# Sliding-window attention: the second query tile's two masked triangles in one block of probabilities

## The chip, the cores and the metric

The kernel runs on one core of a Trainium2 chip. The metric is the device time of one execution in microseconds. Before the change it is 873.5 us, the median of 3 runs (873.45 to 874.37).

## The reference

Layer norm, then grouped-query attention times the silu of a feed-forward block, added to the input. The attention is what the change touches (4 batches of 256 tokens, 32 query heads, 8 KV heads, width 128, window 128):

```python
q = _rope((x @ wq).reshape(B, S, 32, 128), pos)
k = _rope((x @ wk).reshape(B, S, 8, 128), pos)
v = (x @ wv).reshape(B, S, 8, 128)
scores = jnp.einsum('bqhgd,bshd->bhgqs', qg, k) * sm_scale
allowed = (j <= i) & (j > i - 128)
attn = jax.nn.softmax(jnp.where(allowed, scores, neg), axis=-1)
out = jnp.einsum('bhgqs,bshd->bqhgd', attn, v).reshape(B, S, 32 * 128)
return out @ wo
```

A batch is two query tiles of 128. For the first only its own keys count, on and below the diagonal. For the second the keys of the first tile count above the diagonal (the far triangle) and its own on and below it. The two triangles are complementary: together they fill one 128x128 block.

## The kernel before, in words

Five engines run programs of their own, joined by semaphores; the order in each is written out by hand. The feed-forward block takes the first 225 us. Then 8 KV groups follow; a group is two **steps**, one for each pair of batches: `step(g, 0)`, called even below, and `step(g, 1)`, called odd. Groups 1 to 6 are a hardware loop; groups 0 and 7 have small differences, and the last step (`not more`) an order of its own.

Matrix products are exact to nearly 32 bits: an operand is split in a high part (ScalarE, fp32r) and the low rest (VectorE or GpSimd, a subtraction), and `three` (L975) makes three matmuls of each pair.

A step does, for its pair (`b` is the batch in it):
- **the projections of the step to come** (`project`, L1074): 0 is k, 1 is v, 2 to 5 are the four query heads, 12 matmuls each. Rotary embedding of part c: ScalarE swaps halves (`halves`, L482), VectorE multiplies by the cosine (`cos_part`, L788), GpSimd multiplies by the sine and adds (`sin_part`, L316), ScalarE and VectorE split (`kq_hi`, L491; `kq_lo`, L799). On ScalarE and VectorE these stand between the parts of the attention.
- **scores** (L1095): for each head 128x128 for the first tile, 128x256 for the second, in one bank, [own | far, near]. `masking` (L808) takes one bank at a time, adds masks, scales and finds the extreme in two fused operations; `exps` (L512) is on ScalarE; `normalise` (L826) multiplies by the reciprocal sums on VectorE. `scores` of head s waits until head s-2 is masked.
- **turns** (`p_turn`, L1108): the probabilities of four heads are transposed, block by block (r = 0, 1, 2) into a bank; ScalarE copies the high part to `ph[r]` (`p_hi`, L528) and VectorE subtracts the low part `pl[r]` (`p_lo`, L835). The first turn of a batch waits for `probs_done` of all four heads.
- **attend** (L1126): output tile 0 is V0 x block 0, output tile 1 is V0 x block 1 + V1 x block 2. Then `o_hi`, `o_lo` (L534, L846) split the output.
- **out_project** (L1142): 12 matmuls for each of 4 token tiles, into the two banks that `attend` used too. The first waits until `o_lo` of output tile 2 has read its bank. `accumulate` (L852) adds to the running sum.

Queue order decides. Around the change it is: TensorE: turns (0,0) (0,1), projection 0, turn (0,2), projection 1, attend 0, scores, projection 2, scores, turn of V, projections 3 and 4 with turn (1,0) ahead of 4's last part, turn (1,1), projection 5 with turn (1,2) inside, attend 1, scores of the next step, output projections. ScalarE, late in the step: `halves(3)`, `p_hi(1,1)`, `kq_hi(1)`, `p_hi(1,2)`, `kq_hi(2)`, `halves(4)`, `kq_hi(3)`, `o_hi(2)`, `o_hi(3)`, `kq_hi(4)`, exponentials. GpSimd: `sin_part(0)`, in an even step four splits of `wo`, `sin_part(1..4)`, in an even step six splits of the next group's input weights (`lo_in`). Loads go through a ring of 5 slots that these splits set free.

## Time and profile before

| what | value |
|---|---|
| median of 3 runs | 873.5 us |
| the profiled execution | 874.13 us |
| its span, first to last instruction | 872.3 us |
| TensorE busy | 840.8 us (96%) |
| VectorE / ScalarE / GpSimd busy | 597.1 / 472.3 / 390.2 us |
| transposes of `probs` (L1122) | 384 |

Busy time is a sum over instructions. Matmuls overlap: one of 512 columns is shown with 0.39 us, but the next begins 0.23 us after it, so pitches are read from start to start. In the loop all steps of a kind last the same to 0.02 us, so one of each is enough. An idle time stands in brackets behind a row, with the engine that ended it. A row of a stretch reads: from:to, length, then busy us and number of instructions for PE (TensorE), PEld (its weight loads), DVE (VectorE), ACT (ScalarE) and POOL (GpSimd), then the granted clock as a share of 2.4 GHz, the share of the DMA engines and GB/s.

### The profile page before, as it was taken

Reading aid. Unit: us, or ns where it says so; the run is one execution under the profiler, and the core shown is the slowest. Engines: PE = TensorE matmul, PEld = TensorE weight load, DVE = VectorE, ACT = ScalarE, POOL = GpSimd, SP = SyncE. Lnnn points to the kernel's source line nnn. Section 1 sums busy time; section 2 is a strip of 40 time slices with the busy share of each in tenths; the row PEclk is TensorE's granted clock in tenths of the full one; section 3 lists DMA queues with packets and bytes.
Section 4 is the critical chain, followed back from the end, with each engine's and each line's share of the span. In section 5 each row is a group of like instructions: output and inputs, shape, how many; then the busy total and the mean of one; then the engine's idle time right before and its main releaser. Section 6 shows DMA issues by size and latency. Waiting matters only on the chain.

```text
span 872.3 us, 13995 instructions
## 1 busy us (share of the span) xinstructions
PE 840.8 (96%) x4252; PEld 702.3 (81%) x4252; DVE 597.1 (68%) x1615; ACT 472.3 (54%) x1139; POOL 390.2 (45%) x303
## 2 busy tenths in 40 slices
PE   3999999999989999999999999999999999999987
PEld 3777888888767888888888888888888888888876
DVE  7953554433569676876868596777759686866794
ACT  2474121132667557574757575475747566664742
POOL 0144121124545536551744454275525545641893
PEclk9999999999999999999999999999999999999989
DMA  6200001002010201200120102012001201100121
GB/s 195 57 15 10 12 25 46 24 1 72 1 31 19 74 0 49 65 10 1 48 72 0 48 19 54 0 48 72 0 4 44 72 0 48 49 23 0 49 62 72
DMA packets 40224, 32.55 MB, mean 37 GB/s; under 512 B 5056, under 2 KB 32384, under 8 KB 40192
## 3 DMA queue, kind: packets, MB, share of 16 engines
q1 hardware_dynamic: 40192, 32.16, 13.0%
q8 instruction: 16, 0.26, 0.1%
q14 instruction: 16, 0.13, 0.0%
HBM read 30.05 MB, written 2.10 MB: 37 GB/s over the span
## 4 chain that ended last, share of the span: by engine, by line
PE 86%; DVE 6%; ACT 3%; issue 2%; POOL 2%; DMA 0%; SPq 0%; ACTq 0%; DVEq 0%; POOLq 0%
PE bank L982 26%; PE bank L984 25%; PE bank L983 25%; PE bank L1122 5%; PE bank L1102 3%; DVE probs L831 1%; ACT W2raw L434 1%; POOL acc L338 1%; PE bank L1092 1%; PE bank L1002 1%; DVE xl L667 1%; POOL swap L321 1%; DMA xn<-in_L_attn_x 0%; POOL q L325 0%; ACT W2h L435 0%
## 5 line engine op out<-in xcount | busy, mean ns | idle before, releaser
L321 POOL TENSOR_TENSOR swap<-swap,cst 128x512 f32<-128x512 f32 x80 | 103.7, 1296 | 251.1 <-ACT swap L489 249.8
L982 PE MATMUL bank<-xh,wih 128*128 128x512 f32 x384 | 158.0, 411 | 0.2 <-DVE q L795 0.2
L984 PE MATMUL bank<-xh,wil 128*128 128x512 f32 x384 | 150.7, 393 | 0.0
L983 PE MATMUL bank<-xl,wih 128*128 128x512 f32 x384 | 150.0, 391 | 0.0
L516 ACT ACTIVATE probs<-probs,nmx 128x128 f32<-128x128 f32 (+1 forms) x256 | 113.5, 444 | 36.5 <-DVE nmx L816 36.1
L831 DVE TENSOR_SCALAR probs<-probs,rinv 128x128 f32<-128x128 f32 x250 | 125.4, 544 | 4.4
L532 ACT ACTIVATE ph<-bank 128x512 fp32r<-128x512 f32 x96 | 55.7, 598 | 109.5 <-PE bank L1122 108.1
L982 PE MATMUL bank<-woh,oh 128*128 128x512 f32 x256 | 101.1, 395 | 0.0
L983 PE MATMUL bank<-wol,oh 128*128 128x512 f32 x256 | 100.5, 393 | 0.0
L984 PE MATMUL bank<-woh,ol 128*128 128x512 f32 x256 | 100.5, 393 | 0.0
L287 POOL TENSOR_TENSOR hl<-act_h,hh 128x512 fp32r<-128x512 f32 x22 | 29.9, 1363 | 148.1 <-ACT hh L417 148.1
L325 POOL TENSOR_TENSOR q<-q,swap 128x512 f32<-128x512 f32 x64 | 89.3, 1396 | 8.1 <-DVE q L795 3.8
L837 DVE TENSOR_TENSOR pl<-bank,ph 128x512 fp32r<-128x512 f32 x96 | 64.6, 687 | 40.4 <-ACT ph L532 40.2
L984 PEld LDWEIGHTS bank<-xh,wil 128*128 128x128 f32 x384 | 72.1, 188 | 16.0
L305 POOL TENSOR_TENSOR wil<-raw,wih 128x512 fp32r<-128x512 f32 x48 | 61.1, 1305 | 51.1 <-ACT wih L471 51.1
L983 PEld LDWEIGHTS bank<-xl,wih 128*128 128x128 f32 x384 | 72.5, 189 | 11.8
L982 PEld LDWEIGHTS bank<-xh,wih 128*128 128x128 f32 x384 | 72.3, 188 | 12.0 <-DVE q L795 0.6
L816 DVE CUSTOM_DVE_ANT_0 probs<-bank,cst 128x128 f32<-128x128 f32 (+1 forms) x256 | 76.3, 349 | 5.1 <-issue 5.1
L982 PE MATMUL bank<-xh,W13h 128*128 128x512 f32 x176 | 70.5, 401 | 3.4 <-DVE W13l L692 2.4
L848 DVE TENSOR_TENSOR ol<-bank,oh 128x512 fp32r<-128x512 f32 x64 | 43.3, 687 | 40.4 <-ACT oh L537 40.4
L984 PE MATMUL bank<-xh,W13l 128*128 128x512 f32 x176 | 69.2, 393 | 0.0
L983 PE MATMUL bank<-xl,W13h 128*128 128x512 f32 x176 | 68.7, 391 | 0.0
(103 smaller groups left out, 1832.3 us busy)
## 6 DMA issues: line engine op xcount, KB each, us to landing
raw<-in_L_attn_wq SPq DMA_DIRECT2D x32, 256.0 KB, 2.9
raw<-in_L_attn_wo SPq DMA_DIRECT2D x32, 256.0 KB, 2.9
packed<-in_L_ffn_w SPq DMA_DIRECT2D x20, 128.0 KB, 2.1
xn<-in_L_attn_x SPq DMA_DIRECT2D x8, 256.0 KB, 3.4
raw<-in_L_attn_wk SPq DMA_DIRECT2D x8, 256.0 KB, 3.0
raw<-in_L_attn_wv SPq DMA_DIRECT2D x8, 256.0 KB, 2.6
raw<-in_L_attn_x SPq DMA_DIRECT2D x8, 256.0 KB, 2.8
out<-gate SPq DMA_DIRECT2D x8, 256.0 KB, 2.0
```

The source lines that it names most:

```text
L305: nc.gpsimd.tensor_tensor(lo, raw[:, slot, :], hi.bitcast(f32), ALU.subtract).then_inc(wl_done, 1)
L321: nc.gpsimd.tensor_tensor(v, v, spread(sin.unsqueeze(1), P, 2, SEQ), ALU.mult).then_inc(sin_done, 1)
L325: nc.gpsimd.tensor_tensor(dst, dst, swap[:, s, :], ALU.add).then_inc(rope_done, 1)
L516: e = nc.scalar.activation(probs[:, s, c0:c1], probs[:, s, c0:c1], ACT.Exp, bias=nmx[:, s, i:i + 1], scale=-1.0, accum_out=rsum[:, s, i:i ...
L532: nc.scalar.activation(ph[:, r, :], T_B[(7 * bp + j) % 2][:, :], ACT.Copy).then_inc(ph_done, 1)
L816: m = nc.vector.tensor_tensor_reduce(out=probs[:, s, c0:c1], in0=S_B[s % 2][:, c0:c1], in1=mask[:, c0:c1], scale=-SM, scalar=TOP, op0=ALU. ...
L831: m = nc.vector.tensor_scalar(probs[:, s, c0:c1], probs[:, s, c0:c1], rinv[:, s, i:i + 1], None, ALU.mult)
L837: nc.vector.tensor_tensor(pl[:, r, :], T_B[(7 * bp + 4 * b + r) % 2][:, :], ph[:, r, :].bitcast(f32), ALU.subtract).then_inc(pl_done, 1)
L982: nc.tensor.matmul(out_, sh, mh, start=(i == 0), stop=False)
L983: nc.tensor.matmul(out_, sh, ml, start=False, stop=False)
L984: m = nc.tensor.matmul(out_, sl, mh, start=False, stop=(i == n - 1))
L1122: i = nc.tensor.transpose(T_B[(7 * bp + j) % 2][:, h * P:(h + 1) * P], probs[:, 4 * b + h, r * P:(r + 1) * P], ident)
```

## The change

The scores of the second tile are merged before masking: with a predicated copy the far block's scores are written over the near block's wherever the key's index in its tile is above the query's, in PSUM. Softmax, normalise and turn then deal with one block of 128 columns instead of 256. A step has four turns instead of six. Since the one block P holds far and near, the output is taken as V0 x P + (V1 - V0) x (P kept where near): V's second tiles are stored as the difference `vd`, and GpSimd multiplies `ph[1]` and `pl[1]` with a 0/1 mask (`near`) to give block 2. `attend` still has nine matmuls for a batch; before the last three it waits for `kept`.

The order changes too: turn (1,0) goes ahead of part 1 of projection 4 (it was ahead of part 3) and turn (1,1) ahead of its part 3; on ScalarE `p_hi(1,1)` goes ahead of `halves(3)`; GpSimd gets `near(0)` at the start of the step and `near(1)` between `sin_part(2)` and `sin_part(3)`; the first two of the six input splits go ahead of `halves(4)` and `sin_part(4)`. In the last step GpSimd has `near(0)`, `rest(3)`, `rest(4)`, `near(1)` and then the old order. The diff, cut to its core:

```diff
+        causal, plain, far, keep = [cst[:, C_MASK + n * P:C_MASK + (n + 1) * P] for n in range(4)]
+        ident = cst[:, C_ID:C_ID + P]
...
-        probs = sb("probs", [P, 2 * GH, 3 * P], f32, main)
+        probs = sb("probs", [P, 2 * GH, 2 * P], f32, main)
+        vd = sb("vd", [P, 2, HD], f32, main)
...
+            def near(g, bp, b):
+                m = spread(keep.unsqueeze(1), P, GH, P)
+                for p_, s_, out_ in ((ph, ph_done, ph), (pl, pl_done, pl)):
+                    pool.wait_ge(s_, cnt(4, g, bp, 2 * b + 2))
+                    wait(pool, o_ps, cnt(4, g, bp, 2 * b))
+                    nc.gpsimd.tensor_tensor(out_[:, 2, :].rearrange("p (h n) -> p h n", h=GH),
+                                            p_[:, 1, :].bitcast(f32).rearrange("p (h n) -> p h n", h=GH), m,
+                                            ALU.mult).then_inc(kept, 1)
...
+                near(g, bp, 0)
...
-                for c in range(1, 5):
-                    sin_part(ng, nbp, c)
+                sin_part(ng, nbp, 1)
+                sin_part(ng, nbp, 2)
+                near(g, bp, 1)
+                sin_part(ng, nbp, 3)
+                if nxt:
+                    lo_in(g + 1, 0)
+                    lo_in(g + 1, 1)
+                sin_part(ng, nbp, 4)
                 if w and last:
-                    for t in range(4):
+                    for t in range(3):
                         rest(t)
                 if nxt:
-                    for c in range(6):
+                    for c in range(2, 6):
...
+                wait(act, vdl_done, cnt(1, g, bp, 0))
+                tiles = t_bank[:, :].rearrange("p (t n) -> p t n", n=HD)
+                nc.scalar.activation(vd[:, :, :], tiles[:, 1::2, :], ACT.Copy)
+                nc.scalar.activation(vh[:, bp, 0::2, :], tiles[:, 0::2, :], ACT.Copy).then_inc(vh_done, 1)
+            def vd_hi(g, bp):
+                act.wait_ge(vd_done, cnt(1, g, bp, 1))
+                nc.scalar.activation(vh[:, bp, 1::2, :], vd[:, :, :], ACT.Copy).then_inc(vdh_done, 1)
...
-                for r in range(3):
+                for r in range(2):
...
+                v_hi(ng, nbp, T_B[(5 * bp + 2) % 2])
                 halves(ng, nbp, 2)
                 kq_hi(ng, nbp, 0)
+                vd_hi(ng, nbp)
                 p_hi(g, bp, 1, 0)
+                p_hi(g, bp, 1, 1)
                 halves(ng, nbp, 3)
-                p_hi(g, bp, 1, 1)
                 kq_hi(ng, nbp, 1)
-                p_hi(g, bp, 1, 2)
                 kq_hi(ng, nbp, 2)
+                if nxt:
+                    hi_in(g + 1, 0)
+                    hi_in(g + 1, 1)
...
             def masking(g, bp, b, h0):
-                wait(dve, pT_ps, cnt(6, g, bp, 3 * b - 3))
+                wait(dve, pT_ps, cnt(4, g, bp, 2 * b - 2))
                 for h in (h0, h0 + 1):
                     s = 4 * b + h
+                    own, both = S_B[s % 2][:, 0:P], S_B[s % 2][:, 2 * P:3 * P]
                     dve.wait_ge(scores_ps, cnt(8, g, bp, s + 1))
-                    nc.vector.memset(pace[:, s:s + 1], 0.0)
-                    for i, (c0, c1) in enumerate(((0, P), (P, 3 * P))):
+                    nc.vector.memset(pace[:, 2 * s:2 * s + 1], 0.0)
+                    nc.vector.copy_predicated(both, far.bitcast(i32), S_B[s % 2][:, P:2 * P]).then_inc(merged, 1)
+                    dve.wait_ge(merged, cnt(8, g, bp, s + 1))
+                    nc.vector.memset(pace[:, 2 * s + 1:2 * s + 2], 0.0)
+                    for i, (src, add) in enumerate(((own, causal), (both, plain))):
                         m = nc.vector.tensor_tensor_reduce(
-                            out=probs[:, s, c0:c1], in0=S_B[s % 2][:, c0:c1], in1=mask[:, c0:c1], scale=-SM,
-                            scalar=TOP, op0=ALU.add, op1=ALU.min, accum_out=nmx[:, s, i:i + 1])
+                            out=probs[:, s, i * P:(i + 1) * P], in0=src, in1=add, scale=-SM, scalar=TOP,
+                            op0=ALU.add, op1=ALU.min, accum_out=nmx[:, s, i:i + 1])
                     m.then_inc(masked, 1)
...
             def v_lo(g, bp, t_bank):
+                tiles = t_bank[:, :].rearrange("p (t n) -> p t n", n=HD)
                 dve.wait_ge(vh_done, cnt(1, g, bp, 1))
-                nc.vector.tensor_tensor(vl[:, bp].rearrange("p t n -> p (t n)"), t_bank[:, :],
-                                        vh[:, bp].rearrange("p t n -> p (t n)").bitcast(f32),
+                nc.vector.tensor_tensor(vd[:, :, :], vd[:, :, :], tiles[:, 0::2, :], ALU.subtract).then_inc(vd_done, 1)
+                nc.vector.tensor_tensor(vl[:, bp, 0::2, :], tiles[:, 0::2, :], vh[:, bp, 0::2, :].bitcast(f32),
                                         ALU.subtract).then_inc(vl_done, 1)
+            def vd_lo(g, bp):
+                dve.wait_ge(vdh_done, cnt(1, g, bp, 1))
+                nc.vector.tensor_tensor(vl[:, bp, 1::2, :], vd[:, :, :], vh[:, bp, 1::2, :].bitcast(f32),
+                                        ALU.subtract).then_inc(vdl_done, 1)
...
+                    v_lo(ng, nbp, T_B[(5 * bp + 2) % 2])
                     cos_part(ng, nbp, 2)
                     kq_lo(ng, nbp, 0)
                     p_lo(g, bp, 1, 0)
+                    p_lo(g, bp, 1, 1)
+                    vd_lo(ng, nbp)
                 cos_part(ng, nbp, 3)
-                p_lo(g, bp, 1, 1)
                 kq_lo(ng, nbp, 1)
-                p_lo(g, bp, 1, 2)
                 kq_lo(ng, nbp, 2)
...
             def p_turn(g, bp, b, r, last):
-                j = 4 * b + r
+                j = 3 * b + r
                 if r == 0:
                     pe.wait_ge(probs_done, cnt(8, g, bp, 4 * b + 4))
-                if j == 5:
+                if j == 4:
                     if last:
-                        pe.wait_ge(pl_done, cnt(6, g, bp, 2))
+                        pe.wait_ge(pl_done, cnt(4, g, bp, 1))
                     else:
                         pe.wait_ge(vl_done, cnt(1, g, bp, 2))
                 else:
-                    wait(pe, pl_done, cnt(6, g, bp, {0: -1, 1: 0, 2: 1, 4: 3, 6: 4}[j]))
+                    wait(pe, pl_done, cnt(4, g, bp, {0: -1, 1: 0, 3: 2}[j]))
                     if j == 1:
                         pe.wait_ge(vl_done, cnt(1, g, bp, 1))
                 for h in range(GH):
-                    i = nc.tensor.transpose(T_B[(7 * bp + j) % 2][:, h * P:(h + 1) * P],
+                    i = nc.tensor.transpose(T_B[(5 * bp + j) % 2][:, h * P:(h + 1) * P],
                                             probs[:, 4 * b + h, r * P:(r + 1) * P], ident)
                 i.then_inc(pT_ps, 1)
...
+                pe.wait_ge(vdl_done, cnt(1, g, bp, 1))
...
-                    pe.wait_ge(pl_done, cnt(6, g, bp, 3 * b + (1 if t == 0 else 3)))
+                    pe.wait_ge(pl_done, cnt(4, g, bp, 2 * b + t + 1))
                     three(O_B[j % 2][:, :], [(vh[:, bp, 2 * b + kt, :], vl[:, bp, 2 * b + kt, :],
-                                              ph[:, r, :], pl[:, r, :]) for r, kt in blocks]).then_inc(o_ps, 1)
+                                              ph[:, r, :], pl[:, r, :]) for r, kt in blocks],
+                          {1: lambda: pe.wait_ge(kept, cnt(4, g, bp, 2 * b + 2))}).then_inc(o_ps, 1)
...
-                p_turn(g, bp, 0, 2, not more)
-                if not begun:
                     project(ng, nbp, 1)
                 attend(g, bp, 0)
...
-                    pe.wait_ge(pl_done, cnt(6, g, bp, 2))
-                    v_turn(ng, nbp, T_B[(7 * bp + 3) % 2])
+                    pe.wait_ge(pl_done, cnt(4, g, bp, 1))
+                    v_turn(ng, nbp, T_B[(5 * bp + 2) % 2])
                     project(ng, nbp, 3)
-                    project(ng, nbp, 4, {3: lambda: p_turn(g, bp, 1, 0, False)})
-                p_turn(g, bp, 1, 1, False)
-                project(ng, nbp, 5, {2: lambda: p_turn(g, bp, 1, 2, False)})
+                    project(ng, nbp, 4, {1: lambda: p_turn(g, bp, 1, 0, False),
+                                         3: lambda: p_turn(g, bp, 1, 1, False)})
+                project(ng, nbp, 5)
                 attend(g, bp, 1)
...
-    for n, ok in enumerate((j <= i, j > i, j <= i)):
-        c[:, C_MASK + n * P:C_MASK + (n + 1) * P] = np.where(ok, 0.0, NEG)
+    for n, block in enumerate((np.where(j <= i, 0.0, NEG), np.zeros((P, P)), j > i, i <= j)):
+        c[:, C_MASK + n * P:C_MASK + (n + 1) * P] = block
```

## Rows read from the trace of the kernel before

**Rows 1.** The page's first part: busy us, share of the span, instructions.

```profile
PE 840.8 (96%) x4252; PEld 702.3 (81%) x4252; DVE 597.1 (68%) x1615; ACT 472.3 (54%) x1139; POOL 390.2 (45%) x303
```

**Rows 2.** An odd and an even step: span, busy by engine (count), clock.

```profile
524.28:563.83 39.55, 39.55 (x208) 33.60 (x209) 27.98 (x90) 22.29 (x59) 15.62 (x12) 1.00 0.09 25
563.83:603.22 39.39, 39.39 (x208) 33.12 (x205) 30.86 (x89) 27.48 (x69) 23.73 (x19) 1.00 0.15 41
```

**Rows 3.** Timeline of TensorE around a turn: start us, us, engine, line.

```profile
546.28 0.39 PE L984 MATMUL bank<-xh,wil 128*128 128x512 f32 x1
546.51 0.60 PE L1122 MATMUL bank<-cst,probs 128*128 128x128 f32 x4
...
547.18 0.40 PE L983 MATMUL bank<-xl,wih 128*128 128x512 f32 x1
```

**Rows 4.** Timeline of TensorE, the same odd step: five places.

```profile
537.16 0.38 PE L1102 MATMUL bank<-k,q 128*128 128x128 f32 x2
...
542.18 0.39 PE L982 MATMUL bank<-xh,wih 128*128 128x512 f32 x1
...
543.55 0.60 PE L1122 MATMUL bank<-cst,probs 128*128 128x128 f32 x4
...
551.59 0.39 PE L982 MATMUL bank<-woh,oh 128*128 128x512 f32 x1
...
555.05 0.36 PE L982 MATMUL bank<-kh,qh 128*128 128x256 f32 x1
```

**Rows 5.** Timeline of VectorE, the same odd step.

```profile
537.94 0.29 DVE L816 CUSTOM_DVE_ANT_0 probs<-bank,cst 128x128 f32<-128x128 f32 x1 [0.78 <-issue]
...
538.52 0.29 DVE L816 CUSTOM_DVE_ANT_0 probs<-bank,cst 128x128 f32<-128x128 f32 x1
...
539.07 0.69 DVE L795 TENSOR_TENSOR q<-bank,cst 128x512 f32<-128x512 f32 x1
...
539.87 1.58 DVE L831 TENSOR_SCALAR probs<-probs,rinv 128x128 f32<-128x128 f32 x2
...
542.22 0.55 DVE L831 TENSOR_SCALAR probs<-probs,rinv 128x128 f32<-128x128 f32 x2
...
550.70 0.69 DVE L848 TENSOR_TENSOR ol<-bank,oh 128x512 fp32r<-128x512 f32 x1 [0.24 <-ACT oh L537]
```

**Rows 6.** One line's instructions: count, then duration ns min/median/max.

```profile
L816 DVE CUSTOM_DVE_ANT_0 probs<-bank,cst x256: 278/352/422, 243.2 to 844.8; 128x128 f32<-128x128 f32 x128
```

**Rows 7.** Timeline of GpSimd, the odd step and the start of the even one.

```profile
540.00 1.29 POOL L325 TENSOR_TENSOR q<-q,swap 128x512 f32<-128x512 f32 x1
543.11 1.30 POOL L321 TENSOR_TENSOR swap<-swap,cst 128x512 f32<-128x512 f32 x1 [1.81 <-ACT swap L489]
544.49 1.62 POOL L325 TENSOR_TENSOR q<-q,swap 128x512 f32<-128x512 f32 x1
546.24 1.30 POOL L321 TENSOR_TENSOR swap<-swap,cst 128x512 f32<-128x512 f32 x1
547.62 1.38 POOL L325 TENSOR_TENSOR q<-q,swap 128x512 f32<-128x512 f32 x1
...
572.47 5.05 POOL L305 TENSOR_TENSOR wol<-raw,woh 128x512 fp32r<-128x512 f32 x4
```

**Rows 8.** Timeline of ScalarE, the odd step.

```profile
542.44 0.60 ACT L489 ACTIVATE swap<-bank 64x512 f32<-64x512 f32 x1
...
544.18 0.60 ACT L532 ACTIVATE ph<-bank 128x512 fp32r<-128x512 f32 x1 [0.49 <-PE bank L1122]
...
549.76 0.42 ACT L496 ACTIVATE qh<-q 128x256 fp32r<-128x256 f32 x1
```

**Rows 9.** Two long waits of TensorE in its timeline.

```profile
267.17 0.66 PE L1122 MATMUL bank<-cst,probs 128*128 128x128 f32 x4 [1.79 <-DVE probs L831]
...
843.59 1.97 PE L1122 MATMUL bank<-cst,probs 128*128 128x128 f32 x8 [3.29 <-DVE probs L831]
```

**Rows 10.** The stretch behind the second, with its granted clock.

```profile
845.00:849.00 4.00, 4.00 (x12) 3.23 (x11) 3.69 (x9) 2.93 (x11) 3.92 (x4) 0.50 0.46 140
```

More of the change, by code:

```diff
@@ L41 @@
 ALL_Y = NT * NKV
-C_COS, C_SIN, C_MASK, C_ID, C_W = 0, SEQ, 2 * SEQ, 2 * SEQ + 3 * P, 2 * SEQ + 4 * P
+C_COS, C_SIN, C_MASK, C_ID, C_W = 0, SEQ, 2 * SEQ, 2 * SEQ + 4 * P, 2 * SEQ + 5 * P
 def build(nc, x, wq, wk, wv, wo, w1, s1, w2, s2, w3, s3, const, out):
@@ L70, in build @@
         cos, sin = cst[:, C_COS:C_COS + SEQ], cst[:, C_SIN:C_SIN + SEQ]
-        mask, ident = cst[:, C_MASK:C_MASK + 3 * P], cst[:, C_ID:C_ID + P]
+        causal, plain, far, keep = [cst[:, C_MASK + n * P:C_MASK + (n + 1) * P] for n in range(4)]
+        ident = cst[:, C_ID:C_ID + P]
         raw = sb("raw", [P, RING, D], f32)
@@ L160, in build @@
         vT_done, v_ps, vh_done, vl_done = sem("vT_done"), sem("v_ps"), sem("vh_done"), sem("vl_done")
+        vd_done, vdh_done, vdl_done, kept = sem("vd_done"), sem("vdh_done"), sem("vdl_done"), sem("kept")
         pT_ps, ph_done, pl_done = sem("pT_ps"), sem("ph_done"), sem("pl_done")
@@ L355, in step @@
                 if not more:
-                    for t in range(4, NT):
+                    near(g, bp, 0)
+                    rest(3)
+                    rest(4)
+                    near(g, bp, 1)
+                    add_rest(0)
+                    for t in range(5, NT):
                         rest(t)
@@ L361, in step @@
                     return
+                near(g, bp, 0)
                 if more:
@@ L514, in exps @@
                 act.wait_ge(masked, cnt(8, g, bp, s + 1))
-                for i, (c0, c1) in enumerate(((0, P), (P, 3 * P))):
+                for i, (c0, c1) in enumerate(((0, P), (P, 2 * P))):
                     e = nc.scalar.activation(probs[:, s, c0:c1], probs[:, s, c0:c1], ACT.Exp,
@@ L522, in weigh @@
                 act.wait_ge(rinv_done, cnt(8, g, bp, s + 1))
-                for i, (c0, c1) in enumerate(((0, P), (P, 3 * P))):
+                for i, (c0, c1) in enumerate(((0, P), (P, 2 * P))):
                     m = nc.scalar.activation(probs[:, s, c0:c1], probs[:, s, c0:c1], ACT.Copy,
@@ L551, in _ @@
             v_hi(0, 0, T_B[1])
+            vd_hi(0, 0)
             kq_hi(0, 0, 0)
@@ L580, in step @@
                     return
-                for r in range(3):
+                for r in range(2):
                     p_hi(g, bp, 0, r)
@@ L618, in step @@
                 if nxt:
-                    for c in range(6):
+                    for c in range(2, 6):
                         hi_in(g + 1, c)
@@ L829, in normalise @@
                 dve.wait_ge(rinv_done, cnt(8, g, bp, s + 1))
-                for i, (c0, c1) in enumerate(((0, P), (P, 3 * P))):
+                for i, (c0, c1) in enumerate(((0, P), (P, 2 * P))):
                     m = nc.vector.tensor_scalar(probs[:, s, c0:c1], probs[:, s, c0:c1], rinv[:, s, i:i + 1], None,
@@ L877, in _ @@
             kq_lo(0, 0, 0)
+            vd_lo(0, 0)
             for c in range(2, 5):
@@ L912, in step @@
                     return
-                for r in range(3):
+                for r in range(2):
                     p_lo(g, bp, 0, r)
@@ L1175, in step @@
                     out_project(g, 0, 3)
-                    p_turn(g, bp, 0, 2, True)
                     attend(g, bp, 0)
@@ L1180, in step @@
                     out_project(g, bp, 0, True)
-                    p_turn(g, bp, 1, 2, True)
                     out_project(g, bp, 1, True)
```

25 lines of the change are left out of this document (9 added, 16 removed).

## The prediction

> **What bounds the kernel now.** I read the page's busy lines first: TensorE is busy 840.8 of 872.3 us [rows 1]. The stretches of single steps come next. A step is what one KV group does for one pair of batches; 16 make up the attention. I call the step of batches 0 and 1 even (bp = 0) and that of batches 2 and 3 odd. An odd step takes 39.55 us and an even one 39.39 us, and TensorE is busy in all of both, while GpSimd has 15.62 and 23.73 us of work [rows 2]. So inside the loop every instruction taken from TensorE is time won, and every wait that reaches TensorE is time lost. That is why the third view, the timelines of the four engines over one odd step, matters more than the sums: it shows how early each hand-over arrives. There the reader should see that some arrive almost at the moment of need. `ol` of the third output tile starts at 550.70, lasts 0.69 [rows 5], and TensorE starts the output projection that needs the bank at 551.59 [rows 4].
>
> **The transposes removed.** From the matmul before a turn of four to the second one behind it the timeline goes 546.28 to 547.18 [rows 3]: 0.90 us, less two matmul slots of 0.23, so a turn costs 0.44 us. Two turns of six go in each of 16 steps: 32 x 0.44 = **-14.1 us**. Scores, `attend` (three blocks, nine matmuls) and all else on TensorE keep their number.
>
> **The first late point: the hand-over of probabilities.** The turn p10 (`p_turn(g, bp, 1, 0)`) waits for the normalised rows of all four heads. Before, it sat ahead of the last of the four parts of projection 4, at 543.55; now it sits ahead of the second, which ran at 542.18 [rows 4]. Less the 0.44 of the turn removed upstream TensorE asks for it at 541.74. When are the rows ready?
> - TensorE's scores of head 2 start at 537.16 [rows 4], now 536.72; the mask began 0.78 later (537.94 [rows 5]), now 537.50.
> - Masking one head took 0.58 (537.94 to 538.52 [rows 5]). The second mask shrinks from 256 to 128 columns: 0.42 to 0.29. The merge (a predicated copy of 128 columns, PSUM to PSUM) isn't in the trace. At least it costs nothing; at most it is a 256-column mask, 0.42. I take the 128-column mask, nearest in size and memory: a slot of 0.21. On top VectorE must wait for its own merge to end, and a second small memset follows: 0.15 together. That is 0.58 - 0.13 + 0.21 + 0.15 = 0.80 per head, two heads end at 539.10.
> - From the rotation's cosine product (539.07) to the end of the last normalise (542.22 + 0.55) it is 3.70 us [rows 5]. 1.03 of it is the second operation on `probs` standing still while GpSimd adds (1.58 for two against 0.55; the add runs from 540.00 to 541.29 [rows 5, 7]). The add follows the cosine product as before, so this stays. Three second halves shrink by 0.07 each: 3.5, so the rows are ready at 542.6.
> - GpSimd's next multiply began 0.08 after ScalarE's copy at 542.44 had ended [rows 7, 8]. That copy now ends about 0.5 earlier, so the multiply starts at 542.52, in the middle of the last normalise. If that normalise's second operation loses, it is held for 1.29 and the rows are ready at 543.9.
> TensorE waits 0.9 or 2.2 us in an odd step; I take 1.6. In an even step the split of `wo` holds the first normalise, all is 0.2 later, and the collision is nearly sure: 2.2. Ends: 0.9 and 2.5. 8 even and 7 odd steps have it (the last step has its own order): 8 x 2.2 + 7 x 1.6 = **+28.8 us**.
> The Trainium skill ("SBUF — State Buffer", "Who interferes with whom") says that a VectorE instruction with at most one SBUF input, outside the two-port modes, doesn't contend with GpSimd. The merge has one SBUF input, its predicate; by this rule GpSimd never holds it. The masks, also with one SBUF input, agree: of 256 none took longer than 0.422 [rows 6], beside whatever GpSimd ran. Were the merge held as a normalise is, two of them at 1.3 in 15 steps would add 39 us.
>
> **The second late point: `near` in GpSimd's queue.** Call the start of p10 A. Its partner p11 runs two matmul parts later, A + 0.44 + 2 x 0.685 = A + 1.81. ScalarE starts the copy 0.63 behind a turn (543.55 to 544.18) and takes 0.60 [rows 4, 8]: `ph` at A + 3.05. Only then can `near` start, and behind it in the same queue stand rotation 3 and rotation 4. A GpSimd operation on 512 columns has a pitch of 1.38 (546.24 to 547.62 [rows 7]), `near` is two of them: A + 5.85. For TensorE that is early enough, it asks for the kept block at A + 7.1; and the `near` of the first tile has 3 us to spare, so the added wait itself is hidden. But rotation 3 (a multiply and an add) now ends at A + 8.6, where it ended 5.45 after p10 before. Behind it on ScalarE is `kq_hi` of head 2, and behind that `o_hi(2)`, which frees the bank for the output projection. From that `kq_hi` to the projection it was 549.76 to 551.59, 1.83 [rows 4, 8]. So the projection can start at A + 10.45. TensorE asks for it at 551.59 - 543.55 = 8.04, plus 1.37 because p10 is two parts earlier, less 0.44: A + 8.97. The wait is 1.5. VectorE's subtractions with both inputs in SBUF get between the GpSimd operations and push them by up to 0.35 each (an add at 544.49 took 1.62 [rows 7]); with both of them it is 2.1. I take 1.7, ends 1.4 and 2.2: 15 x 1.7 = **+25.5 us**.
>
> **The third: two weight splits moved ahead of rotation 4.** In the 7 even steps with a next group, two operations at 1.26 (5.05 for four [rows 7]) stand between rotations 3 and 4. Their ScalarE halves start long before, their loads are in time (the ring's slots come free at the step's start), so only GpSimd counts. Rotation 4 ends at A + 8.8 + 2.5 + 2.7 = A + 14.0; `kq_hi` (0.42 [rows 8]) and a subtraction as long follow. TensorE wants that operand 3.46 behind the projection's start (551.59 to 555.05 [rows 4]), A + 8.97 + 1.7 + 3.46 = A + 14.1: a wait of 0.85, ends 0.5 and 1.5. What they give back is at the step's end, where VectorE's normalise was held by six splits; with four, but all of it later, I estimate 0.2 more there. With 0.2 for masks and the longer merge ahead of scores 3, in 14 steps: 7 x 0.85 + 14 x 0.2 = **+8.8 us**.
>
> **Costs that I set at nothing.** The value difference `vd` (one more ScalarE copy, one more VectorE subtraction, split in halves): at most one 512-column subtraction, 0.69 [rows 5], behind the hand-over and ahead of `attend` by 4 us; its cover is projection 5. Exponentials and normalise on fewer columns: less work off the path. One block of constants more in the first load (64 KB): zero to 0.3 us. The two turns gone relieve ScalarE and VectorE by 0.6 and 0.69 each; neither was waited for there.
>
> **The last step.** 0.9 of the turns is in the sum. `near` now interrupts GpSimd's products with `gate`, which come later by about 2.7 us: the second `finish` then holds `attend` by about 1 us. Against it, at 843.59 TensorE had waited 3.29 us for a normalise that these products held [rows 9]; with three of them instead of more ahead that shrinks by 2 to 3 us, and the low clock behind it partly. Together **-2.0 us**, ends -4 and +1.
>
> **Sum.** -14.1 + 28.8 + 25.5 + 8.8 - 2.0 = +47.0 us. The profiled execution took 874.13 us (span 872.3 and 1.8 around it); 921.1, and as the median lies 0.6 lower, 920.5: **920 us**. With all lower ends (15.1, 21, 3.5, -4) it is +21.5, 895; with all upper ends (37.5, 33, 13.3, +1) +70.7, 944.
>
> **Rivals.**
> - *One of the two big waits is covered.* If `o_hi(2)` isn't held by rotation 3, 25.5 and 6 fall away: 874 - 14.1 + 28.8 + 2.8 - 2 = 889. If instead the rows are ready for p10: 892. For it: queue orders leave some freedom that I estimated by tenths. Against: each chain is at least 0.9 us too long. Chance 0.15.
> - *The clock falls.* Behind the wait of 3.29 us the granted clock was 0.50 for some 5 us [rows 10], which cost about 2.8 us of work at half speed; behind one of 1.79 us [rows 9] it stayed at full speed. Waits of 2.2 lie between. If it falls in the 8 even steps: +22, 942; in all 15, 962. Chance 0.10.
> - *Faster: TensorE stays full.* The place is p10. If the last normalise ends 0.9 us sooner than I have it (no hold by GpSimd's add and a free merge give 1.4), p10 is on time; and if rotation 3 also gets through before `near`, only the transposes count: 874 - 14 = 860. It decides from the point where TensorE's wait in a step is below the 0.88 it saves. For it: TensorE is full now and the work removed is real. Against: the hold by the add is in every step, and rotation 3 is behind `near` in the program. Chance 0.06.
> - The forecast, within 895 to 944, has the remaining 0.69.
> About 0.2% is what a measurement of this kernel can tell. Faster 0.05, same 0.02, slower 0.93. For 8 times in 10 the range takes in the covered cases in part and stops short of the clock in all steps: 886 to 945.
>
> **What would show it.** In the timeline after: 256 transposes of `probs` where there were 384; idle time of TensorE ahead of them, released by VectorE's normalise, 25 to 35 us in all; idle time ahead of the output projection released by `ol`, 20 to 30 us; steps of about 42 us (odd) and 43.5 us (even); GpSimd busy some 85 us longer and `near` at 1.3 us each. The merge at about 0.3 us. I am wrong if steps are at 38.6 us, if the wait ahead of the projection is missing, or if the kept block itself is what TensorE waits for.

## The result, and the profile after

The changed kernel takes 908.4 us (median of 4 runs, 908.0 to 909.4) against 873.6 before: 34.9 us slower, ratio 1.040 with a 95% interval of 1.0386 to 1.0413. The forecast was 920, with a range of 886 to 945.

First the page's span and busy times of the kernel after (as in [rows 1]).

```profile
span 907.6 us, 13953 instructions
PE 835.7 (92%) x4124; PEld 691.1 (76%) x4124; DVE 608.2 (67%) x1871; ACT 442.9 (49%) x1139; POOL 474.8 (52%) x367
```

The span grew by 35.3 us, while TensorE's busy time fell by 5.1 and GpSimd's grew by 84.6 (85 had been forecast). TensorE's share fell from 96% to 92%: it waits now. Where, the view of its waits says (us in total, times, longest).

```profile
PE bank L1026 <- DVE ol L893: 21.2, 15, 1.5
PE bank L1166 <- DVE probs L869: 13.3, 15, 2.4
PE bank L1037 <- DVE xn L695: 12.4, 2, 10.2
PE bank L1026 <- DVE gate L911: 3.2, 2, 2.9
...
PE bank L1026 <- DVE ql L836: 2.5, 7, 0.4
```

Line 1166 is the turn of `probs`, line 1026 a product in three parts, whose wait for `ol` is the output projection. The two waits of the forecast are there, in 15 steps each. Before, no step waited for `ol`, and of these turns only that of the first step waited (1.79 us [rows 9], now 2.4). The same stretches as [rows 2], an odd and an even step, and then the last 76 us (the columns: from and to, length, busy time and count of PE, PEld, DVE, ACT and POOL, clock, DMA share, GB/s).

```profile
540.81:582.06 41.25, 39.11 (x201) 32.80 (x201) 28.95 (x106) 20.50 (x59) 18.59 (x14) 1.00 0.04 12
582.06:623.93 41.87, 39.28 (x199) 32.42 (x197) 31.78 (x105) 25.40 (x69) 31.39 (x24) 1.00 0.17 50
831.44:907.60 76.16, 60.60 (x301) 49.89 (x298) 46.60 (x153) 32.38 (x93) 58.43 (x45) 0.94 0.17 52
```

Steps are 1.70 and 2.48 us longer than in [rows 2], with less TensorE work in them. In the whole, the second to the fourteenth of the 16 steps account for 27.0 us, what lies ahead of them for 3.8, and the last stretch (the last two steps), 71.7 before, for 4.5. Together 35.3.

TensorE's two waits in the odd step, and the turn's in the even one:

```profile
559.07 0.66 PE L1166 MATMUL bank<-cst,probs 128*128 128x128 f32 x4 [0.76 <-DVE probs L869]
569.56 0.50 PE L1026 MATMUL bank<-woh,oh 128*128 128x512 f32 x1 [1.38 <-DVE ol L893]
600.11 0.66 PE L1166 MATMUL bank<-cst,probs 128*128 128x128 f32 x4 [0.77 <-DVE probs L869]
```

The profile counts idle time from a modelled end. By the distance of the starts, against the same pair of instructions where nothing is waited for, each wait is 0.16 us longer: 0.92 for the turn, in both kinds of step, and 1.54 for the projection.

How the second comes about is seen on GpSimd, in the same odd step (line 324 is a rotation's multiply, 328 its add, 343 `near`, first `ph`, then `pl`):

```profile
559.01 1.29 POOL L324 TENSOR_TENSOR swap<-swap,cst 128x512 f32<-128x512 f32 x1 [1.46 <-ACT swap L514]
560.42 1.60 POOL L328 TENSOR_TENSOR q<-q,swap 128x512 f32<-128x512 f32 x1
562.26 1.29 POOL L343 TENSOR_TENSOR ph<-ph,cst 128x512 fp32r<-128x512 f32 x1 [0.24 <-ACT ph L563]
563.51 1.48 POOL L343 TENSOR_TENSOR pl<-pl,cst 128x512 fp32r<-128x512 f32 x1
564.95 1.47 POOL L324 TENSOR_TENSOR swap<-swap,cst 128x512 f32<-128x512 f32 x1
566.50 1.34 POOL L328 TENSOR_TENSOR q<-q,swap 128x512 f32<-128x512 f32 x1
```

Rotation 2 ends at 562.02, `near` takes 2.7 us, rotation 3 ends at 567.84. ScalarE has stood still for it, and VectorE for ScalarE:

```profile
567.88 0.42 ACT L521 ACTIVATE qh<-q 128x256 fp32r<-128x256 f32 x1 [1.66 <-POOL q L328]
568.20 1.06 ACT L568 ACTIVATE oh<-bank 128x512 fp32r<-128x512 f32 x2
568.81 0.69 DVE L893 TENSOR_TENSOR ol<-bank,oh 128x512 fp32r<-128x512 f32 x1 [1.50 <-ACT oh L568]
```

That is the forecast's chain, link by link. One figure in it deserves a second look: `near` waited for `ph` for only 0.24 us behind rotation 2. Two causes arrive nearly together, and the experiments turn on that.

VectorE in the merge (line 850 is the predicated copy, 854 the masks; of 128 copies none took longer than 0.297 us), and the normalise that GpSimd's add holds:

```profile
550.67 0.29 DVE L850 COPY_PREDICATED bank<-cst,bank 128x128 f32<-128x128 int32 x1
...
551.00 0.29 DVE L854 CUSTOM_DVE_ANT_0 probs<-bank,cst 128x128 f32<-128x128 f32 x1
...
551.21 0.29 DVE L854 CUSTOM_DVE_ANT_0 probs<-bank,cst 128x128 f32<-128x128 f32 x1
...
551.43 0.29 DVE L850 COPY_PREDICATED bank<-cst,bank 128x128 f32<-128x128 int32 x1
...
556.22 1.61 DVE L869 TENSOR_SCALAR probs<-probs,rinv 128x128 f32<-128x128 f32 x2
```

A head takes 0.76 (550.67 to 551.43), where 0.80 was forecast.

### The profile page after: what moved, and what is told of

It reads as the page before. It is cut to its first block, busy times and chain, and to the rows that moved or that the text cites. A ratio compares the mean times of both kernels' runs of the same rounds, so it can differ in the third digit from the quotient of the medians.

```text
span 907.6 us, 13953 instructions
## 1 busy us (share of the span) xinstructions
PE 835.7 (92%) x4124; PEld 691.1 (76%) x4124; DVE 608.2 (67%) x1871; ACT 442.9 (49%) x1139; POOL 474.8 (52%) x367
## 4 chain that ended last, share of the span: by engine, by line
PE 55%; POOL 15%; DVE 14%; issue 10%; ACT 6%; DMA 1%; POOLq 0%; SPq 0%; ACTq 0%; DVEq 0%
PE bank L1026 17%; PE bank L1028 16%; PE bank L1027 16%; POOL swap L324 4%; POOL q L328 3%; DVE probs L869 3%; PE bank L1166 2%; POOL wil L308 2%; DVE q L829 2%; POOL ph L343 2%; DVE ol L893 2%; DVE ql L836 1%; POOL pl L343 1%; PE bank L1146 1%; POOL acc L351 1%
## 5 line engine op out<-in xcount | busy, mean ns | idle before, releaser
L1026 PE MATMUL bank<-xh,wih 128*128 128x512 f32 x384 | 155.9, 406 | 0.0
L324 POOL TENSOR_TENSOR swap<-swap,cst 128x512 f32<-128x512 f32 x80 | 107.3, 1341 | 90.6 <-ACT swap L514 90.6
L1026 PE MATMUL bank<-woh,oh 128*128 128x512 f32 x256 | 101.9, 398 | 21.2 <-DVE ol L893 21.2
L547 ACT ACTIVATE probs<-probs,nmx 128x128 f32<-128x128 f32 x256 | 99.7, 391 | 38.1 <-DVE nmx L854 37.6
L869 DVE TENSOR_SCALAR probs<-probs,rinv 128x128 f32<-128x128 f32 x250 | 112.1, 490 | 4.4
L343 POOL TENSOR_TENSOR ph<-ph,cst 128x512 fp32r<-128x512 f32 x32 | 41.4, 1292 | 127.8 <-ACT ph L563 127.8
L563 ACT ACTIVATE ph<-bank 128x512 fp32r<-128x512 f32 x64 | 36.3, 593 | 97.2 <-PE bank L1166 97.2
L513 ACT ACTIVATE swap<-bank 64x512 f32<-64x512 f32 x80 | 47.6, 595 | 58.5 <-PE bank L1028 58.0
L1026 PEld LDWEIGHTS bank<-woh,oh 128*128 128x128 f32 x256 | 48.2, 188 | 33.4 <-DVE ol L893 14.3
```

The source lines that it names most:

```text
L324: nc.gpsimd.tensor_tensor(v, v, spread(sin.unsqueeze(1), P, 2, SEQ), ALU.mult).then_inc(sin_done, 1)
L343: nc.gpsimd.tensor_tensor(out_[:, 2, :].rearrange("p (h n) -> p h n", h=GH), p_[:, 1, :].bitcast(f32).rearrange("p (h n) -> p h n", h=GH), ...
L513: nc.scalar.activation(swap[0:HALF, a % 2, :], src[HALF:P, :], ACT.Copy)
L547: e = nc.scalar.activation(probs[:, s, c0:c1], probs[:, s, c0:c1], ACT.Exp, bias=nmx[:, s, i:i + 1], scale=-1.0, accum_out=rsum[:, s, i:i ...
L563: nc.scalar.activation(ph[:, r, :], T_B[(5 * bp + j) % 2][:, :], ACT.Copy).then_inc(ph_done, 1)
L869: m = nc.vector.tensor_scalar(probs[:, s, c0:c1], probs[:, s, c0:c1], rinv[:, s, i:i + 1], None, ALU.mult)
```

## The experiments

Ten kernels ran, and the kernel before beside each. The theory at the start was the forecast's: two separate late points, each with its own price. Step lengths below are distances between the transposes of `v`, one in each step; by these the odd and the even step are 41.03 and 42.10 us in the changed kernel, 39.35 and 39.58 before (cut at another place than in [rows 2], with the same sum for a pair to 0.01).

**e1: `o_hi` ahead of `kq_hi(3)` on ScalarE.**

```
                 halves(ng, nbp, 4)
-                kq_hi(ng, nbp, 3)
                 o_hi(g, bp, 2)
                 o_hi(g, bp, 3)
+                kq_hi(ng, nbp, 3)
```

> The changed kernel with one thing moved: on ScalarE the two output splits o_hi(2), o_hi(3) stand ahead of kq_hi(3) instead of behind it. My theory: the wait of 1.54 us in front of the output projection (15 steps) is o_hi(2) standing behind kq_hi(3), which waits for rotation 3, which waits behind near in GpSimd's queue. Then this wait vanishes everywhere; odd steps gain 1.5 us each, but in even steps TensorE only reaches the scores of head 3 sooner and waits there for rotation 4 (2.4 us instead of 0.9), so they gain next to nothing: 908.4 - 7 x 1.5 - 1 = 897 us. Rival: o_hi(2) is late because attend ends late or ScalarE is full, not because of rotation 3: then 908 us.

Measured 899.8 us, ratio 1.0301 (1.0283 to 1.0318). The projection's wait is gone. The odd step falls to 39.72, the even one stays at 42.09: there a new wait stands in place of the old. The kernel's waits of TensorE:

```profile
PE bank L1166 <- DVE probs L869: 13.7, 16, 2.4
PE bank L1037 <- DVE xn L695: 11.9, 2, 9.7
PE bank L1146 <- POOL q L328: 11.1, 7, 1.6
```

In the even steps TensorE next runs into rotation 4, late behind rotation 3, `near` and the two splits.

**e2: the second `near` made small.** It multiplies 4 of 128 columns of each head and leaves out the rest of that product.

```
+                    w_ = P if b == 0 else 4
...
-                                            p_[:, 1, :]..., m, ALU.mult)
+                                            p_[:, 1, :]...[:, :, 0:w_], m[:, :, 0:w_], ALU.mult)
```

> The changed kernel with GpSimd's second near (batch 1 of the pair) multiplying 4 columns of each head instead of 128, which leaves out most of that product; all waits and the order stay. Theory: rotations 3 and 4 come 2.3 us earlier, the wait in front of the output projection (15 x 1.54) vanishes and the one for head 3's scores in even steps nearly (7 x 0.9): 908.4 - 23 - 6 = about 880 us, while the wait of p10 (0.92) stays. Rival: the delay of rotation 3 comes from halves(3) standing behind p_hi(1,1) on ScalarE; then rotation 3 is no earlier and the time stays at 905 to 908 us.

Measured 888.8 us, ratio 1.0161 (1.0144 to 1.0178): 19.6 us less. The wait for `ol` falls to 1.1 us in 6 steps, the turn's stays (13.9 in 16). `near` in the queue is the cause of the projection's wait. A step gains 1.25 and 1.28, not 1.54; 0.27 comes back in the odd step as a wait ahead of two of the scores.

**e3: both turns of the second tile later.**

```
-                    project(ng, nbp, 4, {1: lambda: p_turn(g, bp, 1, 0, False),
-                                         3: lambda: p_turn(g, bp, 1, 1, False)})
+                    project(ng, nbp, 4, {3: lambda: p_turn(g, bp, 1, 0, False)})
+                    p_turn(g, bp, 1, 1, False)
```

> The changed kernel with the two turns of batch 1 back where they were before: p10 ahead of part 3 of projection 4 (instead of part 1) and p11 behind projection 4. Theory: p10 no longer waits (0.92 us in 15 steps gone), but p11 stands only 0.2 us earlier in absolute time, so near, rotation 3 and the bank of the output projection come at nearly the same moment, and the wait in front of the projection grows from 1.5 to 2.2 us: 905 us. Rival: the two waits add up independently, as my sum of the prediction treats them, and 15 x 0.92 comes back: 894.5 us.

Measured 910.3 us, ratio 1.042 (1.0396 to 1.0444), no gain at all. The turn's wait is gone but for the first step (1.1 us), and the projection's has grown by nearly as much. This kernel's waits of TensorE:

```profile
PE bank L1026 <- DVE ol L893: 32.1, 15, 2.2
PE bank L1037 <- DVE xn L695: 11.6, 2, 9.4
```

That explains why so little comes back, but not why nothing does. The steps are 40.72 and 41.80 us long, 0.31 and 0.30 shorter than in the changed kernel, which over 15 steps is the 905 that was expected. In five of the steps, though, the granted clock falls to half within 1.5 us of the end of the wait for `ol`. One of them, a row of TensorE's timeline and a stretch behind it:

```profile
401.41 0.50 PE L1026 MATMUL bank<-woh,oh 128*128 128x512 f32 x1 [2.09 <-DVE ol L893]
```

```profile
402.00:406.00 4.00, 4.00 (x14) 3.14 (x12) 2.94 (x17) 2.06 (x9) 0.28 (x1) 0.57 0.01 2
```

An odd step with such a fall takes 42.19, 1.47 more than one without; the four falls up to the last transpose of `v` cost 4.9 us together. The mean granted clock was 0.977 to 0.985 in the four runs of e3 and 0.992 or 0.993 in those of the changed kernel. So the order gains about 0.3 us a step, and the clock takes it away again.

**e4: the two input splits back behind rotation 4**, on GpSimd and on ScalarE.

```
-                if nxt:
-                    lo_in(g + 1, 0)
-                    lo_in(g + 1, 1)
                 sin_part(ng, nbp, 4)
...
-                    for c in range(2, 6):
+                    for c in range(6):
                         lo_in(g + 1, c)
```

> The changed kernel with the two splits of input weights (ScalarE's and GpSimd's) back at the end of the even step, behind rotation 4, where all six were before. Theory: even steps lose their wait for head 3's scores (0.8 us in 7 steps), and the step's end does not get worse, since VectorE's last normalise is held by four boundaries of GpSimd operations whether four or six of them follow: 903 us. Rival: six splits in a row hold the normalise or the first near of the next step longer, and what is won in the middle is paid at the step's end: 908 to 911 us.

Measured 903.3 us, ratio 1.0328 (1.0311 to 1.0346). The steps are 41.03 and 41.24 long: the even ones have lost 0.86, the others nothing, and the two large waits stand as they were (21.2 and 13.3). This term of the sum is shown by itself.

**e5: the add of rotation 1 made small.** It adds 16 of 512 columns and leaves the rest of the sum out, so it can't hold the normalise.

```
-                nc.gpsimd.tensor_tensor(dst, dst, swap[:, s, :], ALU.add)
+                w_ = 16 if c == 1 else IT
+                nc.gpsimd.tensor_tensor(dst[:, 0:w_], dst[:, 0:w_], swap[:, s, 0:w_], ALU.add)
```

> The changed kernel with GpSimd's add of rotation 1 shrunk from 512 to 16 columns, which leaves out most of that sum; order and waits stay. Theory: this add is what holds VectorE's normalise of head 1 (1.61 us for two operations instead of 0.48). Without it the rows of all four heads are ready 1.1 us earlier, the wait of p10 (0.92 us in 15 steps) vanishes, and since near, rotation 3 and the bank all count from p10's partner, that much comes back in full: 908.4 - 13.8 = 894.6 us. Rival: the probabilities are late because of the masks' two merges alone; then p10 waits on, 905 to 908 us.

Measured 910.0 us, ratio 1.0412 (1.0391 to 1.0433). The expectation of 894.6 fell. The held pair of normalise operations did shrink:

```profile
555.61 0.53 DVE L870 TENSOR_SCALAR probs<-probs,rinv 128x128 f32<-128x128 f32 x2
```

and the turn's wait went with it (1.1 us in 2 steps), but the projection's is now 33.3 us in 15, up to 2.4. GpSimd's timeline tells why:

```profile
558.40 1.31 POOL L324 TENSOR_TENSOR swap<-swap,cst 128x512 f32<-128x512 f32 x1 [2.54 <-ACT swap L515]
559.79 1.63 POOL L329 TENSOR_TENSOR q<-q,swap 128x512 f32<-128x512 f32 x1
561.38 1.57 POOL L344 TENSOR_TENSOR ph<-ph,cst 128x512 fp32r<-128x512 f32 x1
```

`near` starts behind rotation 2's add without a gap. It no longer waits for `ph`. GpSimd is busy from rotation 2's multiply on, and that multiply is tied to TensorE's end of projection 3, by ScalarE's copies. Whoever hurries the turn mostly lets `ph` wait in front of a busy GpSimd. The steps are 40.94 and 41.98 long, about 0.1 shorter than in the changed kernel and not 0.92. The clock fell here too, in five steps, each time around the end of a wait for `ol` of 2.2 or 2.3 us; by the lengths of the steps with and without a fall that cost 6.2 us, so that at full clock this kernel would stand near 904 (an estimate), still far from 894.6. The waits view counts the cause: `near` waited for `ph` 32 times in the changed kernel and 17 times here, which is 15 fewer, once for each step. The first row is of the changed kernel, the second of this one.

```profile
POOL ph L343 <- ACT ph L563: 127.8, 32, 13.3
```

```profile
POOL ph L344 <- ACT ph L564: 129.2, 17, 14.7
```

**e6: no merge.** The predicated copy, its wait and one memset are left out, so softmax takes the near block as it stands and leaves the far triangle out; TensorE still computes the scores of both.

```
-                    nc.vector.copy_predicated(both, far.bitcast(i32), S_B[s % 2][:, P:2 * P])...
-                    dve.wait_ge(merged, cnt(8, g, bp, s + 1))
-                    nc.vector.memset(pace[:, 2 * s + 1:2 * s + 2], 0.0)
```

> The changed kernel without the predicated copy, the wait for it and the second small memset, which leaves the far triangle out of the result. Theory: a head's mask takes 0.33 us less, the two of them ahead of the cosine product 0.66, so the wait of p10 falls from 0.92 to about 0.26 and 15 x 0.66 comes back: 898.5 us. Rival: the masks have slack, because VectorE catches up while GpSimd's add holds it anyway; then 906 to 908 us.

Measured 903.8 us, ratio 1.0349 (1.0329 to 1.0368): about half of what was expected. The turn's wait is all but gone (2.4 us in 2 steps), the projection's rose to 27.5, and `near` waits for `ph` only 18 times: the pattern of e3 (17 times) and e5. The steps are 40.62 and 41.57 long, 0.41 and 0.53 shorter; in two of them the clock fell, which cost 2.3 us.

**e10: two adds small.** The edit of e5 for rotation 2's add as well (`w_ = 16 if c in (1, 2)`), which leaves out most of two sums. It is the test of what e5 seemed to show.

> The changed kernel with the adds of rotations 1 and 2 at 16 columns (leaves out most of two sums). Theory (near(1) starts when GpSimd has finished rotation 2's add, not when ph(1,1) is ready, so the shorter add lets it start about 0.7 us sooner than with rotation 1's add alone shortened): the output projection's wait falls from 2.4 to about 1.7 us in 15 steps, the whole near 899 us. Rival (near(1) starts on ph(1,1), and rotation 2's add has no say): the wait stays at 2.4 us, 908 to 910 us.

Measured 893.4 us, ratio 1.0222 (1.0206 to 1.0238), 15 us below the changed kernel and 5.6 below what was expected. Both kinds of step lose 0.98 (to 40.06 and 41.12), `near` waits for `ph` 32 times again, and the projection's wait is back at the size it had, only the turn's is missing. This kernel's waits of TensorE:

```profile
PE bank L1027 <- DVE ol L894: 21.3, 15, 1.5
PE bank L1038 <- DVE xn L696: 12.6, 2, 10.4
```

The steps show no fall of the clock. With GpSimd free in time, the turn's wait is worth its full 0.92 a step. The direction that e5 left open is shown. The size was expected wrongly because I had taken the 0.7 us of GpSimd as the gain, not the whole way of `ph`.

**e7: order mended in the loop.** The edits of e1 and e4, and the turn of part 0 ahead of part 2, that of part 1 ahead of part 3.

> Three moves together in the changed kernel, nothing left out: o_hi(2), o_hi(3) ahead of kq_hi(3) on ScalarE, all six input splits back at the end of the even step, and p10 ahead of part 2 of projection 4 (p11 stays ahead of part 3). Theory: p10 then waits only 0.25 us, the bank of the output projection is free in time, rotation 4 ends about when scores 3 ask for it (0.2 us); a step takes 38.95 us instead of 41.25 and 41.87, 908.4 - 7 x 2.3 - 8 x 2.9 = 869 us. Rival: with these waits gone the next one is just behind them (the kept block for attend, or rotation 4 behind near, which cannot be later than before by 2.7 us without cost): steps of 40 us or more, 880 us and up.

Measured 880.0 us, ratio 1.0075 (1.0056 to 1.0095). By the distances of the starts the turn's wait fell to 0.24 us and the projection's to about 0.4, but the steps stand at 39.44 and 39.65, where 38.95 had been expected.

**e8: e7, and the last step's GpSimd queue.** `add_rest`, which adds a finished product and is needed only for the output, goes behind the products that TensorE's next work needs; one moves into the step before.

```
+                    add_rest(1)
+                    rest(5)
                     near(g, bp, 1)
-                    add_rest(0)
-                    for t in range(5, NT):
-                        rest(t)
-                        add_rest(t - 4)
-                    for t in range(4, NT - 1):
+                    rest(6)
+                    rest(7)
+                    for t in range(2, NT - 1):
                         add_rest(t)
```

> As the kernel with the three moves, and the last step's GpSimd order changed: add_rest(0) at the end of the step before, then near(0), rest(3), rest(4), add_rest(1), rest(5), near(1), rest(6), rest(7), add_rest(2 to 6). Theory: the changed kernel ends 4 us behind TensorE's last matmul more than before, because GpSimd does four add_rest in a row at the very end, and attend 1 of the last step waits 1.7 us for the finish that needs rest(5). Both shrink: 4 us less than the kernel with the three moves, 865 us. Rival: loads of the last rows, not GpSimd's order, set the end: within 1 us of the other kernel.

Measured 876.8 us, ratio 1.0035 (1.0023 to 1.0046): 3.2 us under e7. Only a small part is for the reason expected: the kernel still ends 7.1 us after TensorE's last matmul (6.6 in e7). A wait of 1.94 us ahead of the last `attend` is gone, but another of 1.2 has come, and TensorE's waits in the last two steps together fell only from 5.9 to 5.4. The rest of the gain goes with the clock (a mean of 0.990 to 0.992 in the runs of e7, of 0.993 to 0.995 in those of e8). In e7 it fell twice in the last step; these two stretches are of e7, the third of e8, where it stayed up until TensorE was done:

```profile
850.00:854.00 4.00, 4.00 (x18) 3.19 (x17) 1.47 (x4) 2.00 (x5) 2.24 (x2) 0.69 0.02 6
862.00:866.00 4.00, 3.90 (x11) 3.08 (x12) 1.29 (x3) 0.60 (x1) 3.92 (x4) 0.59 0.35 131
```

```profile
862.00:866.00 4.00, 4.00 (x20) 3.26 (x18) 1.47 (x3) 0.60 (x1) 3.92 (x4) 1.00 0.00 0
```

**e9: the turns later still, `o_lo` first on VectorE.** e8 with the turns as in e3, and:

```
+                o_lo(g, bp, 2)
                 if more:
                     cos_part(ng, nbp, 4)
-                o_lo(g, bp, 2)
-                kq_lo(ng, nbp, 3)
                 o_lo(g, bp, 3)
+                kq_lo(ng, nbp, 3)
```

> The merged block kept, all orders around it written anew: o_hi(2) and o_hi(3) first on ScalarE, the two input splits back behind rotation 4, the turn of part 0 ahead of part 3 and that of part 1 behind projection 4, o_lo(2), cos_part(4), o_lo(3), kq_lo(3) ahead of the masking on VectorE, and the last step's GpSimd order of the run before (876.8 us). Theory (the turns were the last waits, and work of TensorE put ahead of them covers them): a step loses p10's 0.24, the output projection's 0.27 and about 0.3 of the scores' wait, steps near 38.8 us, the whole near 866 us, ratio 0.99. Rival (GpSimd's queue from rotation 2's multiply to rotation 4's add just becomes the bound, so that what is taken from the turns comes back at the projections or the scores): 875 to 877 us, with waits for q of rotation 4 or for o_l in most steps.

Measured 871.1 us (870.1 to 871.7, 7 runs) beside 873.7 of the kernel before, ratio 0.9971 (0.9960 to 0.9982), faster than both kernels. The edit of the turns gained nothing in the time of e3; here `o_hi` no longer stands behind rotation 3 and the clock doesn't fall in the loop, which would explain the difference, though five edits stand together and were not parted. Two successive steps of it:

```profile
535.77:574.77 39.00, 38.97 (x201) 32.71 (x200) 28.75 (x107) 22.55 (x64) 23.70 (x18) 1.00 0.06 16
574.77:614.00 39.23, 39.19 (x201) 32.61 (x200) 31.40 (x107) 24.05 (x66) 26.17 (x20) 1.00 0.18 52
```

TensorE shows 0.07 us of idle time in the 78.23. A pair of steps is 0.71 shorter than the 78.94 of [rows 2]: 0.35 a step, where two turns are worth 0.88. The rest is in the distances of the starts. The two scores that stand inside the output projections take 1.74 and 1.67 us here where they took 1.16 and 1.17 before, so 0.58 and 0.50 are lost there. 39.35 - 0.88 + 0.58 = 39.05, measured 39.00; 39.58 - 0.88 + 0.50 = 39.20, measured 39.23. Each of these scores waits until VectorE has masked the one two before it, and the merge makes the masks longer. So the merge seems to give back more than 0.5 us of the 0.88 that it earns; that it is the cause was argued from the trace and not shown, as no run took the merge out of this kernel.

Nor did the kernel before run with these orders. In its loop TensorE was busy all of the 39.55 us of a step [rows 2], so an order alone had nothing in sight to win there, and that is where e9 gains: from the second to the fourteenth step it takes 508.6 us and the kernel before 513.0. What the new order of the last step would give the kernel before was not tried.

## Why the prediction came out right

The direction, both mechanisms and the range held; 920 was 11.6 too high. In the profiled executions the sum to meet is 35.3 us, against +47.0. By the terms:

- *Transposes, -14.1.* 128 fewer. That TensorE can get shorter by them is borne out by e9, where the account of a step closes to 0.05 us.
- *The hand-over, +28.8.* Measured 15 x 0.92 = 13.9 (13.3 us of idle time in the view of the waits, where 25 to 35 had been announced; steps of 41.25 and 41.87 instead of 42 and 43.5). This is the mis-sized term. The forecast gave 0.9 or 2.2 and took between them, and 2.2 for even steps, on a collision of the last normalise with GpSimd's next multiply. It never came: the multiply starts at 559.01, the very moment when the last normalise ends (558.53 + 0.48), because ScalarE's copy had only just let it go. The 0.9 was computed right, from rows; what was added to it was a guess about a margin of 0.1 us, and the trace of before could not decide it. The merge's price in it (0.80 a head, 0.76 measured) and the hold of the normalise (1.61) were right.
- *The second late point, +25.5.* Measured 15 x 1.54 = 23.1. The bare chain had given 1.5; of the 0.2 added for VectorE's interference 0.04 came. e2 shows `near` as its cause, e1 the queue on ScalarE that carries it.
- *The third, +8.8.* 7 x 0.86 = 6.0 by e4, and about 1 us for small waits ahead of the scores. That the 0.85 met the 0.86 is partly luck: its own figures (14.0 + 0.42 + 0.42 against 14.1) give 0.7.
- *The last step, -2.0.* What is left for the start and the end is 35.3 + 14.1 - 13.9 - 23.1 - 7 = +5.4. 0.7 us is TensorE's first matmul, at 10.23 instead of 9.49; that is scatter, as it began between 9.1 and 10.8 in the kernels of the experiments, which have the same first load. 4.3 is the end of GpSimd's queue: TensorE's last matmul ends 8.2 us before the span does, and 3.9 before it in the kernel before. The wait of 3.29 us for the normalise [rows 9] is gone altogether: the same turn, now at 872.38, waits for nothing. In its place the first `attend` of this step waits 2.91, for the `finish` that the forecast had put at about 1 us, and the second one 1.74:

```profile
879.09 0.47 PE L1026 MATMUL bank<-ph,vh 128*128 128x512 f32 x1 [2.91 <-DVE gate L911]
```

The clock fell behind the wait of 2.91 as it had behind that of 3.29. The end of the kernel after, on GpSimd:

```profile
897.83 1.29 POOL L355 TENSOR_TENSOR acc<-acc,raw 128x512 f32<-128x512 f32 x1
899.08 5.37 POOL L361 TENSOR_TENSOR gate<-gate,acc 128x512 f32<-128x512 f32 x4
```

Four adds in a row with nothing of TensorE beside them: TensorE ends at 899.4, the span at 907.6. The forecast counted the products delayed by `near`, not the adds piled up behind them. No run took these adds away; e8 only reordered them, and the end behind TensorE stayed nearly as long (7.1 us).

The 11.6 us by which 920 was too high are the difference of larger errors: the hand-over was put 14.9 too high and the last step 7.4 too low. That they partly cancel was luck.

One thing the forecast had wrong without paying for it: it measured the second late point from the start of the turn (A), as if the turn were its only cause, so that a turn on time would save both. GpSimd has a second way into it, from projection 3 by way of rotation 2, which in this kernel is 0.24 us earlier. So its first rival ("the rows are ready for p10: 892") would have needed two things at once: e3 and e5 had the rows ready for the turn, gained 0.3 and 0.1 us a step by it and with the falls of the clock stayed at 910; e10 did both and came to 893. The other half of that rival (`o_hi(2)` isn't held, 889) was tried in e1 and gave 899.8, since rotation 4 came in its place.

As for the rule in the Trainium skill ("SBUF — State Buffer", "Who interferes with whom") that a VectorE operation with at most one SBUF input, outside the two-port modes, is left alone by GpSimd: the 128 predicated copies, 0.283 to 0.297 us each beside whatever GpSimd ran, agree with it.

## What to carry to other kernels

Where a new operation goes into an in-order queue, follow everything behind it to the next engine's queue, and there to the next: TensorE waited for `near` itself only once (0.7 us, in the first step), the work standing behind it was waited for in 15. A wait has the price of its last cause only when the next cause is far behind; read how long the waiting instruction stood (0.24 us here), because the removal of the one cause gives little more than that: 0.1, 0.3 and 0.4 to 0.5 us a step in e5, e3 and e6, and not 0.92. Where two executions differ by less than was expected, read the granted clock of every step before naming a cause. And when a saving is lost to waits, the orders of the neighbouring queues are the place to look: five edits that only reorder took 37 us off the changed kernel, and with them it is 0.3% faster than the kernel before, which has not run with them.

## What the runs showed of the hardware

- A predicated copy from PSUM to PSUM, 128x128 with its predicate in SBUF, takes 0.29 us, as long as the 128-column mask.
- The pair of normalise operations took 1.61 us where a GpSimd add of 512 columns ran beside it and 0.53 with an add of 16 columns; the add ran from 556.26 to 557.55, the pair ended at 557.83. GpSimd's own operations went from 1.29 to between 1.47 and 1.63 in places where VectorE's subtractions ran.
- Behind TensorE's wait of 2.91 us in the last step of the changed kernel, in the second of these stretches, the granted clock fell. It had also fallen in the first step, behind a wait of 2.04 us that ended at 245.10 (third stretch); the same wait was 1.76 in the kernel before, and no fall followed.

```profile
876.00:880.00 4.00, 1.09 (x4) 0.48 (x3) 3.36 (x6) 1.36 (x4) 3.92 (x4) 1.00 0.00 0
880.00:884.00 4.00, 3.73 (x16) 3.14 (x15) 1.69 (x4) 2.26 (x5) 1.96 (x2) 0.63 0.02 6
246.00:250.00 4.00, 4.00 (x14) 3.33 (x15) 3.52 (x26) 2.45 (x12) 0.00 (x0) 0.57 0.01 2
```

- The length of the one wait doesn't decide alone. In e3 the clock fell in five of the 15 steps that wait 2.1 or 2.2 us for `ol`, in e5 in five of those with 2.2 to 2.4 and in e6 in two of those with 1.9; behind the changed kernel's wait of 2.37 at 267.49, and behind e8's of 2.99 in the last step, it stayed at 1.00. In the changed kernel's own loop, with waits of 0.92 and 1.54, it never fell, so the rival of a clock that falls in the steps did not occur there. One fall cost an odd step of e3 1.47 us.
